# Edge sums over 32 destinations in four column strips, three table sets, and 304 of 784 edge tiles counted into panels

## The reference

```
layer 0:  summed = segment_sum(x[src], dst, n);  agg = summed / max(deg_in, 1)
          out = concat([x, agg]) @ weight;  out = out / norm(out) + bias
          x = layernorm(x + out)
layer 1:  h = x * rsqrt(deg_out);  m = segment_sum(h[src], dst, n) * rsqrt(deg_in)
          x2 = m @ W_gc + b_gc + x @ W_res + b_res
          core = top-2 mixture of 64 experts on x2 (gelu MLP, capacity 1024)
          y = batchnorm(x2 + core);  x = layernorm(x + y)
```

## Time and profile before

| | us |
|---|---|
| median of 3 runs | 2371.81 |
| lowest and highest | 2362.14, 2375.26 |
| the profiled execution, its own time | 2364.18 |
| its span in the trace | 2362.4 |
| first sums of layer 0 to those of its last step's end | 60.8 to 830 |
| the same in layer 1 | 931.5 to 1621 |

### The profile page before, as it was taken

The page is one execution under the profiler, slowest core; times in us unless marked ns, Lnnn a source line. Parts: engine busy times, 40 slices in busy tenths (PEclk is TensorE's granted clock), DMA queues, the critical chain, the costliest instruction groups (busy, mean ns, idle before and its releaser), DMA issues.

```text
span 2362.4 us, 49715 instructions
## 1 busy us (share of the span) xinstructions
PE 1978.1 (84%) x15386; PEld 1746.5 (74%) x15386; DVE 1389.2 (59%) x3693; ACT 448.6 (19%) x1261; POOL 1471.3 (62%) x1418
## 2 busy tenths in 40 slices
PE   2899999999998473799999999987744989999847
PEld 1788888888998452698889899976633778878635
DVE  6878777867785387556665665523661333333295
ACT  0211221112210054000000000002321222222227
POOL 5777777767777664777777777773773444444400
PEclk9999999999999796999999999987877999999959
DMA  5344443434433504333333333362314796466873
GB/s 175 112 126 126 116 117 112 122 101 121 130 96 110 167 0 142 112 110 114 110 110 112 104 108 114 104 204 76 50 30 143 249 275 195 132 203 195 247 217 109
DMA packets 220192, 312.71 MB, mean 132 GB/s; under 512 B 47442, under 2 KB 165257, under 8 KB 220028
## 3 DMA queue, kind: packets, MB, share of 16 engines
q0 software_dynamic: 61648, 155.25, 22.7%
q1 hardware_dynamic: 103388, 101.82, 13.7%
q10 hardware_dynamic: 54992, 53.49, 7.6%
HBM read 297.96 MB, written 57.83 MB: 151 GB/s over the span
## 4 chain that ended last, share of the span: by engine, by line
PE 52%; DVE 17%; issue 8%; DMA 8%; POOL 6%; DVEq 4%; SPq 2%; ACT 1%; another core or an unknown queue 0%; POOLq 0%; ACTq 0%
PE bank L1020 15%; PE bank L1050 14%; POOL gath L684 4%; DMA acc<-x_scratch,acc 4%; PE bank L1242 4%; PE bank L1251 4%; PE bank L1068 3%; PE bank L1072 3%; DVE oh_lo L1409 3%; PE bank L1143 2%; PE bank L1085 2%; DVE codes L1431 2%; DVEq L1438 2%; DVEq L1462 2%; DVE oh_hi L1409 1%
## 5 line engine op out<-in xcount | busy, mean ns | idle before, releaser
L684 POOL DMA_INDIRECT gath<-in_x_dram,idx_t x512 | 577.7, 1128 | 218.1 <-issue 130.7
L684 POOL DMA_INDIRECT gath<-h_scratch,idx_t x512 | 527.9, 1031 | 189.9 <-issue 139.5
L1020 PE MATMUL bank<-onehot,gath 128*128 128x128 f32 x4096 | 520.3, 285 | 35.8 <-DMA gath<-h_scratch,idx_t 29.2
L1050 PE MATMUL bank<-Y,X 128*128 128x128 f32 x4312 | 536.1, 277 | 0.0
L1050 PEld LDWEIGHTS bank<-Y,X 128*128 128x128 f32 x4312 | 521.1, 193 | 15.4 <-issue 0.9
L1020 PEld LDWEIGHTS bank<-onehot,gath 128*128 128x128 f32 x4096 | 492.0, 198 | 48.0 <-DMA gath<-h_scratch,idx_t 38.9
L1409 DVE TENSOR_TENSOR oh_lo<-iota_lo,lohi_t 128x512 bf16<-128x512 bf16 x392 | 269.1, 687 | 69.7 <-PE bank L1032 58.5
L1443 DVE TENSOR_TENSOR acc<-acc,bank 128x256 f32 x256 | 107.6, 420 | 286.6 <-issue 268.2
L777 POOL DMA_INDIRECT y_scratch<-acc x96 | 97.1, 1012 | 207.7 <-DVE acc L1812 202.7
L1068 PE MATMUL bank<-codes,oh_lo 128*128 128x400 bf16 x408 | 140.7, 345 | 92.9 <-DVE oh_hi L1409 48.1
L1242 PE MATMUL bank<-acc 128*128 128x128 f32 x1552 | 202.8, 285 | 0.5 <-ACT acc L926 0.5
(11 more groups left out here) (231 smaller groups left out, 2246.4 us busy)
## 6 DMA issues: line engine op xcount, KB each, us to landing
acc<-in_L_gnn_w_dram SPq DMA_DIRECT2D x101, 512.0 KB
acc<-in_L_gnn_w_dram ACTq DMA_DIRECT2D x96, 512.0 KB
y_scratch<-zero_s ACTq DMA_DIRECT2D x49, 256.0 KB
y_scratch<-bias_s SPq DMA_DIRECT2D x98, 128.0 KB
Y<-y_scratch SPq DMA_DIRECT2D x14, 896.0 KB, 13.1
acc<-in_L_gnn_b_dram ACTq DMA_DIRECT2D x96, 128.0 KB
gath<-in_x_dram,idx_t POOLq DMA_INDIRECT x512, 2.9
gath<-h_scratch,idx_t POOLq DMA_INDIRECT x512, 2.8
```

Of the source, the lines that this page charges most:

```text
L684: pool.indirect_dma_start(out=gath[:, half, k, :], out_offset=None, in_=table, in_offset=bass.IndirectOffsetOnAxis(ap=idx_t[:, TD + t:TD + ...
L1020: last = pe.matmul(WINB[half][:, (q * DC + c) * WIN:(q * DC + c + 1) * WIN], gath[:, half, k, c * P:(c + 1) * P], onehot[:, half, k, :], s ...
L1050: last = pe.matmul(DB[w % 2][:, c * P:(c + 1) * P], X[:, h, c * P:(c + 1) * P], panel[:, w % 2, h, :], start=(h == 0), stop=(h == NT - 1))
```

## The change

- **Sums.** Each sparse tile gets a one-hot table over `SUB` = 32 destinations from the tile's own first destination. The table is now the stationary operand and the 128x256 gathered rows the moving one; the four tiles of a window write four strips of 32 partitions of one bank (`PARTB`), with no accumulation among them: 8 products a step of 128x32 by 128x256.
- **Placing.** ACT copies the partial sums to SBUF (`keep_part`). DVE makes for each window a 128x128 one-hot shift matrix (`shifts`) from offsets computed once at the start. PE multiplies (`shift`): 4 products of 128x128 a step, in the next step behind its first piece of `dense`. `add_windows` of a step is moved two steps on, to the front of DVE's step.
- **Split of tiles.** 304 dense tiles (panel pairs 58 to 74), 480 sparse ones: 60 steps of 8, not 64. There are 13 groups, a window of steps is 4.
- **Tables.** `oh_lo`/`oh_hi` have three sets (`TABS`).
- **x.** `turn_x` transposes `X` itself; the copies to `xs` are gone.
- **Room.** Some buffers share memory; the load of `bias0` waits for `y_cleared`, the iota `ids_t` moves behind layer 1, and the start has eight small transposes in place of four and one more broadcast product.

```diff
-PANEL_TILES = ((8, 9), (4, 21), (2, 58))
-GROUP_PANELS = ((1, 1, 6), (1, 3, 4), (1, 1, 6), (1, 3, 4), (1, 1, 6), (1, 3, 4), (1, 1, 6), (1, 3, 4), (1, 1, 6),
-                (0, 2, 6), (0, 2, 6))
-WINDOW = 5
+SUB = 32
+TABS = 3
+PANEL_TILES = ((8, 9), (4, 21), (2, 74))
+GROUP_PANELS = ((1, 1, 6),) * 9 + ((0, 2, 6), (0, 4, 4)) * 2
+WINDOW = 4
...
+            sp.wait_ge(y_cleared, 16 * NT)
+            sp.dma_start(bias_s[:, :], bcast(bias0)).then_inc(bias0_in, 16)
             load_back(0)
...
-            def copy_xs(L, i):
-                wait_count(act, x_turned, NT * L + i)
-                act.activation(xs[:, :], X[:, i, :], ACT.Copy).then_inc(xs_ready, 1)
...
+            def keep_part(L, st):
+                g = ST * L + st
+                act.wait_ge(pairs_done, GROUP // 2 * (g + 1))
+                wait_count(act, shift_done, g - 1)
+                act.activation(part_s[:, st % 2, :, :].rearrange("p q d -> p (q d)"), PARTB[:, 0:WINS * D],
+                               ACT.Copy).then_inc(part_ready, 1)
...
             def sums(L, st):
                 g = ST * L + st
                 half = st % 2
                 pe.wait_ge(onehot_ready, g + 1)
-                if st >= 2:
-                    pe.wait_ge(acc_step, acc_sparse[L][st - 2])
+                wait_count(pe, part_ready, g)
                 for k in range(GROUP):
                     q, t = k // QUAD, k % QUAD
                     pe.wait_ge(gath_full[half * GROUP + k], 16 * (g // 2 + 1))
-                    for c in range(DC):
-                        last = pe.matmul(WINB[half][:, (q * DC + c) * WIN:(q * DC + c + 1) * WIN],
-                                         gath[:, half, k, c * P:(c + 1) * P], onehot[:, half, k, :],
-                                         start=(t == 0 and c == 0), stop=(t == QUAD - 1), skip_group_check=True)
+                    last = pe.matmul(PARTB[SUB * t:SUB * (t + 1), q * D:(q + 1) * D], onehot[:, half, k, :],
+                                     gath[:, half, k, :], start=True, stop=True)
                     if k % 2 == 1:
                         last.then_inc(pairs_done, 1)
 
+            def shift(L, st):
+                g = ST * L + st
+                pe.wait_ge(shift_ready, g + 1)
+                pe.wait_ge(part_ready, g + 1)
+                if st > 0:
+                    pe.wait_ge(acc_step, acc_sparse[L][st - 1])
+                for q in range(WINS):
+                    for c in range(DC):
+                        last = pe.matmul(SHIFTB[:, (q * DC + c) * WIN:(q * DC + c + 1) * WIN],
+                                         part_s[:, st % 2, q, c * P:(c + 1) * P], shift_s[:, st % 2, q, :],
+                                         start=True, stop=True)
+                last.then_inc(shift_done, 1)
...
                 dense(L, st, lo, lo + (hi - lo) // chunks)
+                if st > 0:
+                    shift(L, st - 1)
...
                 v.tensor_tensor(onehot[:, st % 2, :, :],
-                                iota_w[:, :].unsqueeze(1).to_broadcast([P, GROUP, WIN]),
+                                iota_code[:, 0:SUB].unsqueeze(1).to_broadcast([P, GROUP, SUB]),
                                 rel_t[:, GROUP * st:GROUP * (st + 1)].unsqueeze(2)
-                                .to_broadcast([P, GROUP, WIN]), ALU.is_equal).then_inc(onehot_ready, 1)
+                                .to_broadcast([P, GROUP, SUB]), ALU.is_equal).then_inc(onehot_ready, 1)
+
+            def shifts(L, st):
+                g = ST * L + st
+                wait_count(dve, shift_done, g - 1)
+                for q in range(WINS):
+                    last = v.tensor_scalar(shift_s[:, st % 2, q, :], iota_code[:, 0:WIN],
+                                           shift_at[:, WINS * st + q:WINS * st + q + 1], None, ALU.is_equal)
+                last.then_inc(shift_ready, 1)
 
             def degree_one_hots(e, t):
-                wait_count(dve, hist_done, e - 1)
+                wait_count(dve, hist_done, e - TABS + 1)
...
             def add_windows(L, st):
-                dve.wait_ge(pairs_done, GROUP // 2 * (ST * L + st + 1))
+                dve.wait_ge(shift_done, ST * L + st + 1)
...
             def step0(st):
                 e = hist_first[st]
                 u = first_unit[st]
+                if st > 1:
+                    add_windows(0, st - 2)
                 degree_one_hots(e, TD + GROUP * st)
                 for _, t, _ in units_at[st][0:1]:
                     code_one_hots(0, u, t)
                 one_hots(0, st)
                 for _, t, _ in units_at[st][0:1]:
                     degree_one_hots(e + 1, t)
-                if st > 0:
-                    add_windows(0, st - 1)
+                shifts(0, st)
                 add_panels(0, st)
```

More of the change, by code:

```diff
@@ L152, in gnn_kernel @@
         acc_dense.append([])
-        for st in range(ST + 1):
-            if st > 0:
+        for st in range(ST + 2):
+            if st > 1:
                 a += WINS
@@ L878, in _ @@
             in_sevens(act, NT, scale_h)
-            copy_xs(1, 0)
-            for i in range(NT):
-                turned_x(1, i)
-                if i + 1 < NT:
-                    copy_xs(1, i + 1)
+            for st in range(ST):
+                if st < NT:
+                    turned_x(1, st)
+                keep_part(1, st)
             def stage_sums(tiles):
@@ L995, in _ @@
             pe.wait_ge(tabs_made, 3)
-            for k in range(2 * CH):
-                last = pe.transpose(banks[0][0:1, k * P:(k + 1) * P], wmin[:, k:k + 1], ident[:, :])
+            for c in range(CH):
+                for h in range(QUAD):
+                    last = pe.transpose(banks[c][0:1, h * P:(h + 1) * P], wmin[:, QUAD * c + h:QUAD * c + h + 1],
+                                        ident[:, :])
             last.then_inc(wmin_turned, 1)
@@ L1120, in _ @@
                 step(0, st)
+            shift(0, ST - 1)
             def far_sums(L):
@@ L1367, in _ @@
             link(v.tensor_copy(dstN.bitcast(I32), dstT))
-            dve.wait_ge(base_spread, 1)
+            dve.wait_ge(base_spread, 2)
+            for j in range(QUAD):
+                at = slice(SUB * j, SUB * (j + 1))
+                v.tensor_scalar(shift_at[at, :], banks[0][at, 0:ET - TD].rearrange("p (q h) -> p h q", h=QUAD)[:, j, :],
+                                part_col[at, 0:1], float(-SUB * j), ALU.add, ALU.add)
             v.tensor_tensor(relT[:, 0:512], dstT[:, 0:512], banks[2][:, 0:512], ALU.subtract)
@@ L1380, in _ @@
             v.tensor_scalar(far_t[:, :], relT, -1.0, None, ALU.add)
-            link(v.tensor_reduce(small[:, 5:6], tmpT, AX, ALU.add))
+            link(v.tensor_reduce(small[:, 9:10], tmpT, AX, ALU.add))
             dve.sem_inc(tabs_made, 1)
@@ L1615, in step1, with spread_step @@
                 p = NPAN + first_panel[st]
+                if st > 1:
+                    add_windows(1, st - 2)
+                def spread_step():
+                    one_hots(1, st)
+                    shifts(1, st)
+                    if st == 0:
+                        for j in range(4):
+                            dve.wait_ge(h_stored[j], 16 * (NG7 if j < 3 else 1))
+                    if 0 < st <= NT:
+                        add_bias(st - 1)
+                    add_panels(1, st)
                 for k, (w, t, unit_parts) in enumerate(units_at[st]):
@@ L1619, in step1 @@
                     if k == 0:
-                        one_hots(1, st)
-                        if st > 0:
-                            add_windows(1, st - 1)
-                            if st <= NT:
-                                add_bias(st - 1)
-                        else:
-                            for j in range(4):
-                                dve.wait_ge(h_stored[j], 16 * (NG7 if j < 3 else 1))
-                        add_panels(1, st)
+                        spread_step()
                     for part in unit_parts:
```

153 lines of the change are left out of this document (86 added, 67 removed).

## The result

The changed kernel takes 2248.4 us (median of 4 runs, 2243.2 to 2253.1) and the one before 2369.6 in the same comparison: a ratio of 0.949, interval 0.947 to 0.951. The prediction named 2335 us as the likeliest and 2249 us as rival B, with 0.26. The profiled execution has a span of 2249.9 us, 112.5 less than before.

What follows compares the result with a forecast made beforehand. PE was taken to bound both layers, POOL close behind. Layer 0 -36, layer 1 -6, layer ends +5 and start +4 gave -33 us: 2331 from the profiled 2364.2, set to 2335 for run medians; range 2225 to 2405.

Steps and rivals of the forecast that it cites:

- rival B: The four strips stream together, each with its own queue of records: sums 1.2 us a step, 2249 us, chance 0.26.
- The new sums: PE's strip products in a step: one record a tile by program order, 2.1 us in place of 3.65.
- The lower bound: The sums if all four strips stream together: 0.87 us plus 0.33 for filling and imperfect overlap, 1.2 us a step.
- PE's step without its sums: PE's dense, degree, transpose, `prep` and shift products in a step: 10.16 us in layer 0, 9.43 in layer 1.
- The placing term: The four `shift` products on PE add 0.92 us a step, at 0.228 us each.
- The stalls before: PE's stalls in the old kernel's full steps: 0.84 us in layer 0, of which 0.67 idle, and 0.11 in layer 1.
- POOL's pace: Eight gathers with their gaps on POOL: 11.34 us a step in layer 0, 10.65 in layer 1.
- The tails: The last 8 steps of each layer, at 11.8 and 9.82 us a step: 94 and 79 us.
- The start: DVE's some eight more operations on rows before the first steps: +4 us, bounds 0 and 6.
- A: One record a tile in program order: sums 2.1 us, 2335 us in all, POOL waiting 47 us in layer 1, chance 0.42.
- C: Nothing overlaps between strips: sums 3.64 us a step, layer 0 ending at 868 us, 2484 us in all, chance 0.16.
- D: Strips overlap by program order, but hand-overs from DVE and ACT stall PE: likelier 2372 us, chance 0.16.

Runs made afterwards that it cites:

- experiments 2 and 7: The changed kernel with a window's four tiles on two strips in turn: 2288.5 us, one run; and with the four placing products made twice: 2341.0 us.
- experiments 1 to 3: The changed kernel with all tiles on one strip: 2396.1 us; on two strips in turn: 2288.5 us; with the sums' products ordered by strip: 2253.8 us.
- experiment 4: The kernel before with only the new split of tiles and a window of 4 steps, one iota table read from a larger equal one: 2450.1 us, ratio 1.034.
- experiment 6: The changed kernel with two table sets in place of three: 2267.1 us, ratio 0.958.
- experiment 5: The changed kernel with the old split of 272 dense and 512 sparse tiles and a window of 5: 2286.6 us, ratio 0.966.
- experiment 8: The changed kernel with POOL's clearing of `acc` moved ahead of the first gather: 2245.6 us; moved also ahead of the wait for the slot table: 2240.1 us.

## Why the prediction went wrong

**The bound** was right. PE sets the full steps before and after, POOL close behind it; experiments 2 and 7 show it one to one.

**The step that failed** is "The new sums ... the steady distance is one record a tile and not two: 9 x 0.217 = 1.95 us ... 2.1 us". It rested on "PE starts records in program order". Those rows have only products that fill the whole array; they could not show what a product on a strip waits for. Measured is 1.00 us, and experiments 1 to 3 show the rule: a strip runs its own records one behind the other and the strips run side by side. That is rival B's condition, "its own queue of records". The lower bound worked out as 0.87 + 0.33 = 1.2 us was the better value: with the 0.19 us that the change of shape costs outside the sums, they cost PE 1.19 us a step. Over 96 full steps the term is 0.91 x 96 = 87 us too high. The forecast of 2335 missed 2248 by the same 87 us; that the other errors below cancel is luck.

**The rules of the Trainium skill.** The trace disagrees with the program order that I took from the Trainium skill's "TensorE: Matmul & The Clock Gate", Part 3, beside my rows: starts are in order only within a strip. It agrees with the same section in that strips run concurrently, and by more than its 2.38 for three: 3.57 / 1.00 = 3.6 for four strips of 256 columns. For the drain of the Trainium skill's "TensorEngine Tiling (Array Packing)", Key Properties, I had 0.15 us a step. What the traces show around the sums is 0.3 us in all; how much of it is a drain they do not say.

**The other terms.**
- PE's step without its sums: 10.16 and 9.43 us. With 1.00 us of sums and the 0.19 us in their neighbours that leaves stalls of 0.27 and 0.10 us, where I had kept 0.3 and 0.11. The placing term was right (0.89 us against 0.92), and so, as far as this remainder tells, were the dense and build terms; `prep` is 0.10 us dearer than in the earlier trace rows.
- The stalls before: of the 0.84 us a step in layer 0 I had explained the 0.67 of idle time. The lower clock behind the long waits, up to 0.2 us a step by the estimate in experiment 4, can account for the other 0.17.
- The third table set: right in kind, worth 17 us (experiment 6).
- The split: I carried its cost, 1.39 us a step, and the four steps fewer, correctly. Alone it costs 83 us, with the new sums it gains 38.
- POOL's pace: 11.34 and 10.65 us were too high, 10.85 and 10.30 when it is the bound (experiment 5). A gather in layer 0 then takes a mean of 421.32 / 398 = 1.06 us and not 1.118; why was not looked into.
- The tails: eight steps take 74.4 and 69.9 us where I had 94 and 79. In layer 0 I had also taken 830 us as the end of the sums, as the table of times before has it; their last record ends at 819.6.
- The start: "+4 ... bounds 0 and 6" was too small. DVE's preparation ends at 55.35 us and not at 37.05: 10.9 of these 18.3 us are the held cast, 7.4 the operations that I put at 4. Step 4's sums are only 14.6 us later, since before it is a selection table that the clearing holds (experiment 8). Moving the clearing gives 10.9 us back; what the same move would do to the kernel before was not tried, so how much of the 14.6 the collision explains stays open.
- The hand-over at a layer's end: from the last sums to the first product 5.8 and 5.4 us before, 8.2 and 8.8 after. 5.8 us in both layers together, predicted 5.

**The rivals.** B is what happened. That its 2249 lies within a microsecond of the median is luck: faster tails, a slower start and the 15.1 us more behind layer 1 cancel. POOL's wait for PE in layer 1's full steps is 25.4 us, nearer to B's "small" than to A's 47. B's sign that PE's idle time has the gathers' DMA ahead of it did not come: in layer 0 it is `oh_hi` for 14.2 us, all of it, and POOL's pace is not the bound. C is what happens without the overlap (layer 0's end 869.4 us, predicted 868, where a start 21 us later and a tail 23 us shorter cancel). D did not show: no wait of PE in 100 to 640 us names `sums_work`, and the tables cost it 13.5 us in 540.

## What to carry over

Where products have 32 output columns or fewer, put them on four strips of the output's partitions: here 16 float32 records took 1.00 us in place of 3.57, and the order of the products in the program didn't matter. Rows of whole-array products say nothing on that, so when two bounds lie a factor of three apart and only a premise on scheduling decides between them, the premise deserves its own chance. When one engine is relieved, ask which engine is next and whether work can be moved between them: the same split of tiles cost 83 us before the relief and gained 38 after it. Count also what a new shape does to the products beside it: here 0.3 us a step that no row of before could show. And look where a longer preparation ends: here it slid under another engine's long operation, and moving that operation gave 10.9 us.

## What was not expected of the hardware

- Records pass each other between strips: in the order by strip, four starts 12 to 14 ns apart belong to products two places apart in the program, while each strip's next record starts 0.2 us later, and the weight loads carry the semaphores that tell the products apart.
- The start distance within a strip is 0.216 us for 256 columns (0.240 after the first record) whether one, two or four strips are busy with float32 rows.
- Going from whole-array products to strips and back costs 0.3 us a step here, part of it in the products behind, where `prep`'s second record starts 0.320 us after its first and not 0.218.
- Some DVE operations that overlap a POOL clearing of 10.7 us last until it ends: 11.50 us for a cast of 0.57, 9.30 us for a TENSOR_SCALAR of 0.17 (128x8 elements). A TENSOR_TENSOR of 0.35 us and a TENSOR_REDUCE of 1.22 us were not held.
